# Four post-norm layers on one core: the attention's stacked operands in rows eight apart, twelve transfers of 16 rows, and norm_apply in another place

## The reference

```python
x = _layernorm(x + _L0_attn_ref(x, ...))   # 16 heads of 8, with biases
x = _layernorm(x + _L0_ffn_ref(x, ...))    # 8 experts, best two of each token
x = _layernorm(x + _L1_attn_ref(x, ...))   # one head of 128
x = _layernorm(x + _L1_ffn_ref(x, ...))    # token mixing
x = _layernorm(x + _L2_attn_ref(x, ...))   # 16 heads of 8, causal
x = _layernorm(x + _L2_ffn_ref(x, ...))    # token mixing
x = _layernorm(x + _L3_attn_ref(x, ...))   # linear attention
x = _layernorm(x + _L3_ffn_ref(x, ...))    # 16 experts, best one, limited room
```

```python
def _layernorm(x, axis=-1, eps=1e-05):
    m = jnp.mean(x, axis=axis, keepdims=True)
    v = jnp.var(x, axis=axis, keepdims=True)
    return (x - m) / jnp.sqrt(v + eps)
```

## Time and profile before

| | us |
|---|---|
| median of 3 executions | 1490.85 |
| lowest and highest | 1484.42, 1494.45 |
| the profiled execution | 1494.64 |
| its span in the profile | 1492.9 |
| PE busy | 1116.8 (75%) |
| DVE busy | 949.5 (64%) |
| ACT busy | 611.3 (41%) |
| POOL busy | 466.4 (31%) |
| mean granted TensorE clock | 0.835 |

### The profile page before, as it was taken

The page is one execution under the profiler, slowest core; times in us unless marked ns, Lnnn a source line. Parts: engine busy times, 40 slices in busy tenths (PEclk is TensorE's granted clock), DMA queues, the critical chain, the costliest instruction groups (busy, mean ns, idle before and its releaser), DMA issues.

```text
span 1492.9 us, 32425 instructions
## 1 busy us (share of the span) xinstructions
PE 1116.8 (75%) x9203; PEld 718.6 (48%) x9203; DVE 949.5 (64%) x3482; ACT 611.3 (41%) x1352; POOL 466.4 (31%) x694
## 2 busy tenths in 40 slices
PE   2989889888469995666648988888976898338950
PEld 1334333333258885555425554555544566325730
DVE  3788788776513323997846775777547687761237
ACT  1366555556224442335412554555554232113310
POOL 3122343333524454332431121111024111442553
PEclk9998787778679998899765998999877797558985
DMA  5544444531257768211025343443010000133523
GB/s 160 123 101 108 114 98 97 115 73 31 95 158 204 208 199 260 85 46 40 29 63 122 96 95 93 96 95 88 18 29 28 22 25 11 46 108 93 168 76 92
DMA packets 202232, 142.21 MB, mean 95 GB/s; under 512 B 14977, under 2 KB 190338, under 8 KB 201986
## 3 DMA queue, kind: packets, MB, share of 16 engines
q1 hardware_dynamic: 194946, 126.35, 32.8%
q0 software_dynamic: 7168, 14.37, 2.7%
HBM read 72.42 MB, written 48.58 MB: 81 GB/s over the span
## 4 chain that ended last, share of the span: by engine, by line
PE 47%; DVE 26%; issue 12%; POOL 5%; ACT 5%; DMA 3%; SPq 1%; DVEq 1%; POOLq 0%; ACTq 0%
PE po L1513 7%; PE po L466 6%; DVE mx L635 5%; PE pm L431 5%; DVE xg L336 4%; PE pt L1507 4%; PE pm L1507 4%; PE pm L418 3%; PE p L559 3%; POOL rstd L329 2%; ACT ob L596 2%; DMA xs<-xg 1%; DVE st L317 1%; POOL sorted L1347 1%; DVE mv L320 1%
## 5 line engine op out<-in xcount | busy, mean ns | idle before, releaser
L635 DVE TENSOR_REDUCE mx<-pm 128x2 f32<-128x512 f32 (+1 forms) x512 | 303.6, 619 | 149.3 <-PE pm L431 71.9
L587 ACT ACTIVATE ex<-pt 128x512 f32<-128x512 f32 (+1 forms) x512 | 266.9, 546 | 218.1 <-PE pt L437 137.9
L431 PE MATMUL pm<-ks,qs 48*128 48x256 bf16 (+1 forms) x1024 | 187.0, 275 | 27.0 <-DVE mx L635 24.6
L326 POOL TENSOR_SCALAR ve<-mv 128x2 f32<-128x2 f32 x96 | 25.4, 264 | 569.2 <-DVE mv L320 569.2
L437 PE MATMUL pt<-qs,ks 51*128 51x256 bf16 (+1 forms) x1024 | 179.3, 268 | 0.8 <-ACT ex L587 0.5
L466 PE MATMUL po<-ex,va 128*32 128x256 f32 (+1 forms) x2048 | 169.0, 405 | 12.0 <-ACT ob L596 11.0
L1590 POOL DMA_INDIRECT result<-ye,to_row x128 | 122.5, 957 | 152.7 <-issue 107.0
L431 PEld LDWEIGHTS pm<-ks,qs 48*128 48x128 bf16 x1024 | 76.3, 101 | 123.9 <-issue 67.1
L1513 PE MATMUL po<-he,we 128*128 128x256 f32 (+1 forms) x448 | 112.9, 395 | 0.6 <-DVE yt L1551 0.4
L310 ACT COPY xt<-p 128x256 f32<-128x256 f32 x112 | 41.8, 373 | 165.5 <-PE p L306 142.8
L336 DVE TENSOR_SCALAR xg<-res,mv,rstd 128x128 f32<-128x128 f32 (+1 forms) x192 | 87.5, 497 | 32.4 <-POOL rstd L329 32.2
(11 more groups left out here) (277 smaller groups left out, 2526.8 us busy)
## 6 DMA issues: line engine op xcount, KB each, us to landing
we<-in_pack SPq DMA_DIRECT2D x40, 514.5 KB
xs<-xg SPq DMA_DIRECT2D x112, 128.0 KB
scr<-parts SPq DMA_DIRECT2D x64, 192.0 KB
qs<-scr SPq DMA_DIRECT2D x64, 192.0 KB, 3.8
ks<-scr SPq DMA_DIRECT2D x64, 192.0 KB, 4.4
scr<-parts SPq DMA_DIRECT2D x64, 128.0 KB
we<-in_pack SPq DMA_DIRECT2D x16, 512.0 KB
xe<-sorted SPq DMA_DIRECT2D x56, 132.0 KB
```

The costliest lines, as they stand in the source:

```text
L431: last_m = pe.matmul(mine[:, e * S + k0:e * S + k1], queries, keys[:, k0:k1], start=not causal, stop=e == 1 or not causal)
L587: nc.scalar.activation(ex[j % 2][:, :, :].rearrange("p (e g) k -> p g e k", g=2)[:, 1 - u, :, lo:S], pt[:, u, :].rearrange("p (b k) -> p b ...
L635: nc.vector.tensor_reduce(mx[q.slot % 2][:, qt, u, 2 * b:2 * b + 2], pm[:, u, :].rearrange("p (b k) -> p b k", k=S)[:, :, 0:hi], AX.X, ALU ...
```

## The change

- The row of product c and feature d becomes 8d + c in each half of 64, so one product lies in rows eight apart. Both passes contract all 64 rows. The three rows of the maxima are 6, 14 and 22 of each half. `ks` holds ones in those rows and zero in the other spare ones; `qs` is cleared at the start of each heads stage by POOL (`stack_zero`), and its rows 6, 14, 22, ... get zeros from `zt` for each sequence.
- So that the partitions of `parts` lie in the order of the rows (even heads in the lower half), q and k are projected by `by_half`: two matmuls of 64 columns each, with every other column of the weights. The biases of layer 0 are brought into the same order at the start (`bias`).
- SP's six writes, the wait and four reads become 12 direct transfers from `parts` into 16 rows of a stack, and one of zeros.
- `norm_apply` goes from j == 2 to j == 7 on DVE, and PE's transposes of `xr` from (3, 0) to (3, 1).
- At the start, DVE's eight memsets of `ks` become one reduce, one scale and four copies.

```diff
@@ heads_sync
-                        r = HALF * of_pair + STACK
-                        sp.dma_start(qs[q.slot][r:r + 3, :, :],
+                        r = HALF * of_pair + MAX_AT
+                        sp.dma_start(qs[q.slot][r:r + 2 * DH + 1:DH, :, :],
...
-                    s = q.slot % 2
-                    for c, n_c in ((0, 3), (3, 2), (5, 1)):
-                        sp.dma_start(scr[q.slot, 0, c:c + n_c].rearrange("c p k -> p c k"), parts[s][:, 0:n_c, 0, :]
-                                     ).then_inc(to_scr, 16)
-                        sp.dma_start(scr[q.slot, 1, c:c + n_c].rearrange("c p k -> p c k"),
-                                     parts[s][:, 3 - n_c:4 - n_c, 1, :].to_broadcast([P, n_c, S])).then_inc(to_scr, 16)
-                    wait_apart(sp, to_scr, 16 * PRODUCTS * (a + q.n + 1), passed)
-
                     wait_apart(sp, ts_ps, 16 * (a + q.back(3)), passed)
-                    for i, stack in enumerate((qs, ks)):
-                        src = scr[q.slot, i].rearrange("c (d h g) k -> (c d) h g k", h=HP, g=2)
-                        for of_pair in range(2):
-                            r = HALF * of_pair
-                            sp.dma_start(stack[q.slot][r:r + STACK, :, :], src[:, :, of_pair, :]
-                                         ).then_inc(stacked[q.slot], 16)
+                    sp.wait_ge(stack_zero, SLOTS * (1 if a == 0 else 2))
+                    for r, of in enumerate(PAIRS):
+                        for i, stack in enumerate((qs, ks)):
+                            sp.dma_start(stack[q.slot][r::DH, :, :].rearrange("r h k -> r (h k)"),
+                                         parts[q.slot % 2][:, of[i], i, :]).then_inc(stacked[q.slot], 16)
+                    sp.dma_start(qs[q.slot][MAX_AT::DH, :, :].rearrange("r h k -> r (h k)"),
+                                 zt[:, 0:S // 2].bitcast(BF16)).then_inc(stacked[q.slot], 16)
@@ heads_tensor
+        def by_half(dst, left, right):
+
+            for of_pair in range(2):
+                last = nc.tensor.matmul(dst[HALF * of_pair:HALF * of_pair + HALF], left[:, of_pair::2], right,
+                                        start=True, stop=True)
+            return last
...
-                return stack[q.slot][HALF * g:HALF * g + k, at_head, :]
+                return stack[q.slot][HALF * g:HALF * g + HALF, at_head, :]
...
-                        pe.matmul(p1[:, 0:S], mat(f"q{layer}"), xq, start=True, stop=True)
+                        by_half(p1[:, 0:S], mat(f"q{layer}"), xq)
...
-                if routed and (j, u) == (3, 0) and (q := at(6)):
+                if routed and (j, u) == (3, 1) and (q := at(6)):
@@ heads_vector
-                    if j == 2 and (q := at(5)):
-                        norm_apply(dve, q, n)
...
+                    if j == 7 and (q := at(5)):
+                        norm_apply(dve, q, n)
@@ heads_pool
+            for i in range(SLOTS):
+                nc.gpsimd.memset(qs[i][:, :, :].rearrange("p h k -> p (h k)").bitcast(F32), 0.0).then_inc(stack_zero, 1)
@@ start
-            pe.matmul(po0[:, 0:3 * D], ones[0:1, :], row1[:, :], start=True, stop=True).then_inc(rows_ps, 1)
-            pe.wait_ge(rows_sb, len(ROWS))
+            pe.matmul(po0[:, 0:3 * D], ones[0:1, :], row1[:, :], start=True, stop=True)
+            by_half(po1[:, 0:2], ident[:, :], cv[:, 0:2]).then_inc(rows_ps, 1)
+            pe.wait_ge(rows_sb, SPREAD)
...
-                for g in range(2):
-                    nc.vector.memset(ks[i][HALF * g + 32:HALF * g + HALF, :, :].rearrange("p h k -> p (h k)").bitcast(F32),
-                                     float(np.uint32(0x3F803F80).view(np.float32))).then_inc(consts_v, 1)
...
+            for i in range(SLOTS):
+                nc.vector.tensor_copy(ks[i][:, :, :].rearrange("p h k -> p (h k)").bitcast(F32),
+                                      max_row[:, :].to_broadcast([P, HP * S // 2])).then_inc(consts_v, 1)
```

More of the change, by code:

```diff
@@ L134, in post_norm_stack @@
         cv = sb("cv", [P, len(COLS)])
+        bias = sb("bias", [P, 2])
+        max_row = sb("max_row", [P, 1])
         row1 = sb("row1", [1, len(ROWS) * D])
@@ L206, in post_norm_stack @@
             mp = [sb(f"mp{i}", [P, 2, 2, 3, HP], BF16, mem) for i in range(2)]
-            mt = [sb(f"mt{i}", [STACK, S], BF16, mem) for i in range(2)]
+            mt = [sb(f"mt{i}", [6 * HP, S], BF16, mem) for i in range(2)]
             ob = sb("ob", [P, 4, S], F32, mem)
@@ L212, in post_norm_stack @@
             xb = [sb(f"xb{i}", [P, 2, D], F32, mem) for i in range(SLOTS)]
-        PRODUCTS = 6
-        scr = nc.dram_tensor("scr", (SLOTS, 2, PRODUCTS, P, S), BF16).ap()
+        PAIRS = [(0, 0), (1, 0), (2, 0), (0, 1), (1, 1), (0, 2)]
         def psum(name, shape, dt=F32):
@@ L389, in heads_sync, with half @@
             sweep(sp, 7, step, lead=SLOTS if routed else 0)
+        def by_half(dst, left, right):
[3 more added lines that the diff above has]
+            return last
         def heads_tensor(pe, a, g, causal, layer, routed):
-            def half(stack, q, g, k, at_head):
-                return stack[q.slot][HALF * g:HALF * g + k, at_head, :]
+            def half(stack, q, g, at_head):
+                return stack[q.slot][HALF * g:HALF * g + HALF, at_head, :]
             def scores(qt, jt, qm, jm, u):
@@ L427, in scores @@
                     if qm:
-                        keys = half(ks, qm, gm, STACK, 2 * bm + e)
-                        queries = half(qs, qm, gm, STACK, 2 * bm + e)[:, qtile * P:qtile * P + P]
+                        keys = half(ks, qm, gm, 2 * bm + e)
+                        queries = half(qs, qm, gm, 2 * bm + e)[:, qtile * P:qtile * P + P]
                         k0, k1 = (qtile * P, qtile * P + P) if causal else (0, S)
@@ L433, in scores @@
                     if qt:
-                        keys = half(ks, qt, gt, STACK + 3, 2 * bt + e)[:, ktile * P:ktile * P + P]
-                        queries = half(qs, qt, gt, STACK + 3, 2 * bt + e)
+                        keys = half(ks, qt, gt, 2 * bt + e)[:, ktile * P:ktile * P + P]
+                        queries = half(qs, qt, gt, 2 * bt + e)
                         k0, k1 = (ktile * P, ktile * P + P) if causal else (0, S)
@@ L441, in scores @@
                         if qm and qtile == 1:
-                            keys = half(ks, qm, gm, STACK, 2 * bm + e)
-                            queries = half(qs, qm, gm, STACK, 2 * bm + e)
+                            keys = half(ks, qm, gm, 2 * bm + e)
+                            queries = half(qs, qm, gm, 2 * bm + e)
                             last_m = pe.matmul(mine[:, e * S:e * S + P], queries[:, P:S], keys[:, 0:P],
@@ L489, in between @@
                         wait(pe, res_sb, n_of(layer) + q.back(4))
-                        pe.matmul(p1[:, 0:S], mat(f"q{layer}"), xq, start=True, stop=True)
+                        by_half(p1[:, 0:S], mat(f"q{layer}"), xq)
                     else:
-                        pe.matmul(p1[:, S:2 * S], mat(f"k{layer}"), xq, start=True, stop=True).then_inc(qk_ps, 1)
+                        by_half(p1[:, S:2 * S], mat(f"k{layer}"), xq).then_inc(qk_ps, 1)
                 if (j, u) == (1, 1) and (q := at(3)):
@@ L500, in between @@
                     for t in range(2):
-                        last = pe.transpose(p0[0:STACK, S:2 * S].bitcast(BF16)[:, t * P:t * P + P],
+                        last = pe.transpose(p0[0:6 * HP, S:2 * S].bitcast(BF16)[:, t * P:t * P + P],
                                             mp[q.slot % 2][:, t, :, :, :].rearrange("p g c h -> p (g c h)"),
```

31 lines of the change are left out of this document (20 added, 11 removed).

## The result

The changed kernel took 1445.78 us, median of 4 executions (1442.71 to 1455.11), against 1492.65 before (median of 4 with the profiled one); the ratio is 0.9707, 95% interval 0.9648 to 0.9766. Run again later, on another occasion, it gave 0.9733 (0.9693 to 0.9772). The forecast was 1447, in a range of 1424 to 1474. The time came out as forecast, in part by luck: most of the way there did not, as the experiments show.

What follows compares the result with a forecast made beforehand. The prediction took PE, nearly always busy, and its clock, lost in routed steps behind an idle piece, as the bound. Terms of -36, -11, +2, 0, 0, -2 and +1 sum to -46, from 1493 to 1447 us, range 1424 to 1474.

Steps and rivals of the forecast that it cites:

- A: Routed heads: moving norm_apply and the xr transposes frees the norm pair and keeps PE's clock up, -36 us.
- E: Score and mask matmuls: contracting 64 rows instead of 48 or 51 takes the same 0.28 us, so 0.
- the clock of 0.9: Sign of being right: granted TensorE clock of 0.9 or more over the seven full routed steps.
- the steps of 18 to 19: Sign of being right: each of the seven full routed steps takes 18 to 19 us, against 22.2 before.
- PE no longer standing for mx: Sign of being right: PE does not stand for DVE's mx behind the norm pair, before 1.52 us.
- R2: Rival, DVE beside POOL: the long instruction only changes its victim, sel, gap or run; 1478 us, chance 0.08.
- B: Causal heads: the same norm_apply move saves 1.0 us per step for 11 steps, -11 us.
- C: by_half projections: two 64-column matmuls run side by side and cost 0.06 us a step per stage, +2 us.
- D: SP's stack transfers: thirteen issues of 0.45 to 0.82 us leave the queue slack, booked as 0.
- R3: Slower rival: SP's queue becomes the bound if its thirteen issues are dear; 1480 to 1550 us, chance 0.07.
- F: Starts: -2 us at the kernel's start from replacing ks memsets, +1 at the causal start from POOL clearing qs.
- R4: Better rival: no idle piece is left on PE and all slow-clock time goes; 1425 us, chance 0.10.

Runs made afterwards that it cites:

- norm_alone: The kernel before with only norm_apply moved to j == 7 and the xr transposes to (3, 1): 1483.53 us, ratio 0.9947.
- rows_64: norm_alone with both score passes contracting all 64 rows of a half, DRAM scratch and whole projections kept: 1459.69 us, ratio 0.9809.
- rows_48: The changed kernel with both score passes contracting only the first 48 rows of each half: 1477.11 us, ratio 0.9913.
- one_matmul: The changed kernel with q and k each projected by one matmul of 128 columns instead of two of 64: 1454.85 us, ratio 0.9763.
- six_more: The changed kernel with six more transfers of zeros per sequence in SP's queue, behind the thirteen: 1503.32 us, ratio 1.0086.
- sel_early: The changed kernel with the ranking's sel and gap in j == 1, ahead of POOL's rem: 1446.43 us, ratio 0.9699; run again, 1446.20 us, ratio 0.9674.
- run_early: sel_early with run and seen moved to j == 1 too: 1456.30 us, ratio 0.9757.
- norm_back: The changed kernel with only norm_apply back in j == 2: 1466.47 us, ratio 0.9814.

## Why the prediction was right, and where it was not

The total of 1447 met 1445.78 by luck: two large errors cancel, 29 us too much from A and 24 too little from E. Of the signs named beforehand, norm's 0.59 in its new place, the causal steps (16.7 for 16.5) and by_half came; the clock of 0.9, the steps of 18 to 19 and PE no longer standing for mx did not, and R2's sign, sel over 1 us with PE waiting behind it, was there.

- **A, -36 for the routed steps by the move: the step that failed** is "I book 0.5 for that", the price of the lock's next victim. It was 1.52 us (sel 1.68 for 0.16), about as much as the norm had lost (1.97 for 0.59), and PE stood 1.45 where it had stood 1.52. norm_alone, 155.50 against 155.30 for the seven steps, shows the term there as zero. What is left of it is 7 us in the three steps without full routing, which was forecast at -7; the last three, forecast at -8, moved by 0.3. This was the rival R2, "the long instruction only changes its victim", given 0.08. Its price, 1478, was near norm_alone's 1483.5. The reason against it, "the small size of sel and gap", was no reason: the earlier trace rows already showed a gap pair of 0.35 taking 1.19, and what is lost is set by POOL's instruction, not by the victim. The Trainium skill ("SBUF — State Buffer", section "Who interferes with whom") says that issue order, not the shape of the instruction, decides who waits. By that rule a small sel is as good a victim as a large one, and the trace agrees, at 1.68 beside 1.17; on the order it does not, since by the profile sel starts 0.46 ahead of rem and is held all the same.
- **E, 0 for 64 rows: the other step that failed.** The matmul's duration is the same, 0.28, and from that I concluded that the rows are free of effect. They win some 24 us when added (norm_alone to rows_64) and cost 22 to 31 when taken away (rows_48), in stretches where the clock falls. This is about half of the gain. Why the clock comes back sooner with more rows stays open.
- **B, -11 for the causal heads.** The mechanism was right. norm_alone wins 8.4 there (278.1 to 269.7 between first and last v product, profile to profile), the rest of the 17 us comes with the stack and the halves. Some 6 of it are there in rows_64, whose clock between the two points is 0.98 for norm_alone's 0.95; but rows_48 has 0.98 too, so that it is the rows is not shown for this stage. In the changed kernel a causal step's norm pair stands at 908.45 and takes 0.59.
- **C, +2: about -3**, in the causal steps (0.15 to 0.2 in each), half of it from shorter matmuls (0.66 for 0.70, two pairs a step).
- **D, 0 for the transfers.** rows_64 (scratch) and one_matmul (direct transfers) differ by 5 us in the total, within the intervals, some 2 of it at the start (first transposes at 55.1 and 53.2). The issue of the new shape took 0.60, within the bounds. That the queue "keeps slack" held, but for the wrong quantity: R3 compared the sum of issues with the step, break-even at 1.17 us each. Six more issues, 4.69 us together, already did it, and the changed kernel is close to that edge: in six_more PE came to the place 4.1 us behind ACT's copy `mt` (940.37, copy at 936.29) and the rows were usable 1.4 behind the end of their issue; in a causal step of the changed kernel the rows are these:

```profile
913.28 0.68 SPq L303 DMA_DIRECT2D xs<-xg  x1
914.08 1.55 SPq L363 DMA_DIRECT2D qs<-mt  x2
```

```profile
913.37 0.37 ACT L607 COPY mt<-p 48x256 bf16<-48x256 bf16 x1 [0.28 <-PE p L503]
```

  The issue ends at 915.63, so they are usable at 917.0, and wanted at 913.37 + 4.1 = 917.5. That is an estimate from these rows, but by it half a microsecond is left; PE goes on there at 917.38 without standing.
- **F, -2 and +1.** The start came out at -2.6. In the causal start POOL's four memsets took 3.77, not 4.6, and held DVE's norm pair for 2.79:

```profile
734.96 2.79 DVE L338 TENSOR_SCALAR xg<-res,mv,rstd 128x128 f32<-128x128 f32 x2 [1.25 <-POOL rstd L331]
```

```profile
734.87 3.77 POOL L736 MEMSET qs<- 128x1024 f32 x4
```

  The stretch that holds this start took 388.3 us in both kernels, so no price of it shows, though that stretch varies by some 7 us between profiles.
- **R4** does not add up as written: -58, -14, 0 and -1 from 1493 give 1420, not 1425, and the bound that it names is -62. It bears on nothing here.

The chain of ratios puts the parts in order, each step one part of the change: 0.9947 with the move, 0.9809 with the 64 rows, 0.9763 with the direct transfers, 0.9707 and 0.9733 with the halves. Only the first two steps are clear of noise: 0.9947 has an interval of 0.9912 to 0.9983, which leaves out 1, and 0.9809 one of 0.9748 to 0.9870, which lies below it. The later ones overlap.

## What to carry to other kernels

When an instruction is moved away from a collision with GpSimd, look at what now stands beside that GpSimd instruction: the loss goes by how much of the GpSimd instruction is left, however small the victim (1.5 us for a sel of 0.16 beside rem, 0.3 for a run of 0.15 late in parts). Move the next one too, as sel_early does, and look at what stands in its new place, as run_early shows. In these kernels a contraction over 48 rows took no less time than one over 64 (0.28), and where TensorE stalled in each step it cost the clock; zero rows that come for nothing may be worth filling in. For a DMA queue, compare the issue of each item with the moment it is wanted, not the sum of issues with the period.

## What the runs showed of the hardware

- The number of contraction rows acts on TensorE's clock. With 64 rows in place of 48 and 51, and nothing else in PE's program different, the mean granted clock of the seven routed steps is 0.85 in place of 0.79 (rows_64 against norm_alone), and 0.87 and 0.85 in place of 0.81 (the changed kernel's two profiles against rows_48). The fall itself comes with either, at a stand of 1.45; what differs is how long the slow piece lasts. The length of the stand alone does not decide it: with 1.85 in norm_back and 64 rows the clock is 0.85 as well. Stages at 1.00 throughout show no difference (67.60 against 67.80; 67.10 against 67.00). Other numbers of rows, and which of them hold zeros, were not tried.
- A VectorE sum of 128x16 with both inputs in SBUF was held 1.5 us beside a GpSimd instruction of 1.17, longer than the instruction itself: in the step shown sel starts 0.46 ahead of rem and ends 0.05 behind it, so the one that starts first by the profile is not the one that goes through. In those 0.46 us GpSimd was still at a scatter:

```profile
199.68 0.96 POOL L1352 DMA_INDIRECT sorted<-xr,place  x1 [0.30 <-issue]
```

  The scatter alone did not hold it: in sel_early the same sum at 214.06, beside a scatter of 1.09 from 213.35, took 0.18. And in the causal step of the earlier trace rows, where GpSimd had been idle for 2.75, the norm pair starts 0.21 ahead of rem (858.66, 1.16) and is held too.
- A VectorE tensor_scalar pair was held 2.2 us beside GpSimd memsets (2.79 for 0.59), which read nothing.
- Two matmuls of 64 columns over the same 256 moving columns, into the two halves of the array, take 0.66 together where one of 128 columns takes 0.70.
- Twelve transfers from 128 partitions into 16 rows eight apart were issued at 0.59 to 0.60 each, now and then 1.1 to 1.9, and showed no limit of their own in any step.
